# A graph kernel on one core: VectorE's sum of two edge types in three parts, and new places for the basis lots

## The chip, the cores and the metric

One Trainium2 chip, one NeuronCore. The time is device microseconds of one execution of the whole kernel, and the median of several executions is what versions are compared by.

## The reference

1536 nodes with 512 features, 26112 edges (`src`, `dst`, a type of 0 or 1, a weight), and four graph layers one after another, each followed by a residual and a layer norm:

```
layer 0: attention over image features, segment_sum of x[src] by dst, two products with W, relu
layer 1: two gated relational steps. For each type r: w[r] = sum over 30 bases of att[r, b] * basis[b],
         out = segment_sum(where(type == 0, gate0 * (x[src] @ w[0]), gate1 * (x[src] @ w[1])), dst) + x @ root + bias
layer 2: five GIN steps, relu((1 + e) * (h @ W) + A @ (h @ W) + b), then log_softmax
layer 3: support = x @ W, out = segment_sum(support[src] * weight, dst) + bias
```

The kernel turns each segment sum into a product with a dense 1536 x 1536 matrix: one of edge counts for each type, their sum for layers 0 and 2, and one of weights for layer 3.

## The kernel before, in words

The change lies in the first stage, which runs from about 20 us to about 320 us. It does two jobs side by side.

**Counting edges.** The 1536 destinations are cut into 96 windows of 16 (`W`), eight windows to a block of 128 (`PER`), twelve blocks (`BLOCKS`). The edges are sorted by destination, so a window needs a few tiles of 128 edges: two in static slots and one or two more in a loop with a count read from the data. For each tile VectorE writes one-hot matrices (`sources` L713, `source` L718, `keys` L722 and L723), and TensorE multiplies them (`counts`, L1483 and L1484) into one of three PSUM rings (`win`). Static slots are used by every second window, the looped slot `looped_slot(w)` too, so a window with a second looped tile needs its slot back from TensorE in the middle. ScalarE evicts a window's counts to `typed` (in the buffer `wb`, L1203) and its weights to `aw_stage` (L1205). When a block's eight windows are done, TensorE turns it in six lots ("turn" lots, L1460 and L1463), and ScalarE writes the turned tiles to `adj` and to `aw_dram`. Once a block VectorE adds both types of `typed` into `adj[:, 0]` (`sum_types`, L708); it does that in the window with index `RING` = 3 of the next block, behind that window's one-hots.

**Combining the bases.** Both relational steps need 2 x 512 x 512 weights from 30 bases. These stream in as 64 chunks of 960 KB (`load_chunk`, L382), and TensorE reduces each in a "basis" lot (L1451, eight matmuls); ScalarE copies every second result to `mixed`, SP writes it to DRAM. There are four chunk buffers (`basis_of`); two lie in rows of `adj` that the last blocks need, so from chunk 52 on only two are used. A chunk's buffer is loaded again by SP as soon as TensorE has read it (`follower`, `side_ps`). Chunks 53 to 63 wait for the chunk that is two before them, earlier ones for that four before.

**The order.** The lots of both kinds form one list `side`; `by_window[u]` says which lots TensorE and ScalarE do behind window u. Turn lots of block s stand in windows q = 1 to 6 of the next block. Basis lots stand in every window with `u % 3 != 2`, so at windows 0, 1, 3, 4, 6, 7 and so on. SP works through chunks in order. It also issues seven small loads (`small`: biases, `Wa`, `eps`), one with each of chunks 8 to 14. After all lots it loads `wf` into `wb`, behind waits for all lots and for all sums. ScalarE waits for the sum of block s - 2 before it overwrites that half of `typed` (`typed_summed`).

Behind the stage come the turned x, the attention, and then the products of the four layers, on TensorE almost without a gap.

Of the kernel before, what the change touches and what calls it, by code (L numbers as in the profile page):

```python
# [6 lines left out]
ALU, ACT, AX = mybir.AluOpType, mybir.ActivationFunctionType, mybir.AxisListType  # L7

P = 128
# [14 lines left out]
RING = 3  # L24
# [8 lines left out]
N_SMALL = 7  # L33
# [10 lines left out]
def program(nc, ins, out):  # L44
    with ExitStack() as ctx:
        def sb(name, shape, dt):
            return ctx.enter_context(nc.sbuf_tensor(name, shape, dt))

        def sem(name):
            return ctx.enter_context(nc.semaphore(name))  # L50


        adj = sb("adj", [P, 3, NT, N], F16)
# [109 lines left out]
        def lay(n, dt, shape_str=None, **kw):  # L163
            nonlocal at
            size = n * (2 if dt in (F16, BF16) else 4) // 2
            v = flat[:, at:at + size]
            at += size
            if dt != F16:
                v = v.bitcast(dt)
            return v.rearrange(shape_str, **kw) if shape_str else v  # L170
# [10 lines left out]
        basis = [flat[:, 0:4 * D * 2].bitcast(F32), lay(4 * D, F32)]  # L181
# [12 lines left out]
        def follower(n):  # L194

            return min([m for m in range(n + 1, 64) if basis_of(m) == basis_of(n)], default=None)
# [20 lines left out]
        def looped_slot(w):  # L217

            return 4 + w % 2

        def static_slots(w):

            return 2 * (w % 2), 2 * (w % 2) + 1
# [3 lines left out]
        typed = wb[:, :, :, :].rearrange("p a b n -> p (a b n)").bitcast(F16)[:, 0:2 * 2 * NT * P].rearrange("p (k m j d) -> p k m j d", k=2, m=2, j=NT)  # L227
        assert 2 * at <= H1 + 7 * 2048

        c_ready = sem("c_ready")  # L230
# [14 lines left out]
        typed_summed = sem("typed_summed")  # L245
# [3 lines left out]
        weights = {k: sem("in_" + k) for k in ("wf", "wi", "img", "wim", "small", "wn", "wt", "wbm", "bap", "ts_a", "ts_b", "ts_in", "root", "l1a", "l1b", "aw", "att", "as_out", "as_in")}  # L249
# [62 lines left out]
        BLOCKS = N // P  # L312
        PER = P // W
        CH = 2 * 32

        side, by_window = [], {u: [] for u in range(NW)}
        for u in range(NW):
            here = []
            s, q = u // PER - 1, u % PER
            if s >= 0 and 1 <= q <= 6:  # L320
                here += [("turn", s, q - 1)]
            if u == NW - 1:
                here += [("turn", BLOCKS - 1, n) for n in range(6)]
            if u % 3 != 2:
                n = 2 * (u // 3) + u % 3
                here.append(("basis", n // (CH // 2), n % (CH // 2)))
            for what in here:
                by_window[u].append((len(side),) + what)
                side.append(what)
        lot_of = {what: n for n, what in enumerate(side)}  # L330

        def evicted(w):

            return win_free[w % RING], w // RING + 2
# [17 lines left out]
        def side_copied(n):  # L352

            return len([m for m in range(n + 1) if leaves(m)])
# [20 lines left out]
        def _(sp):  # L375
# [3 lines left out]
            def load_chunk(n):  # L379
                l, c = n // (CH // 2), n % (CH // 2)  # L380
                c = c // 2 + 16 * (c % 2)
                sp.dma_start(basis[basis_of(n)][0:120, :], bases[l][:, c * (4 * D):(c + 1) * (4 * D)]).then_inc(basis_in[basis_of(n)], 16)  # L382

            sp.wait_ge(edges_in, 64)
            for n in range(3):
# [4 lines left out]
            small = [  # L390
                (bcol[:, 0:2], ins["L0_gnn_bf"].rearrange("(k p) -> p k", p=P)),
                (bcol[:, 2:4], ins["L0_gnn_bi"].rearrange("(k p) -> p k", p=P)),
                (bcol[:, 4:5], ins["L0_gnn_ba"].unsqueeze(0).broadcast_to([P, 1])),
                (wa[:, :], ins["L0_gnn_Wa"].rearrange("(k p) o -> p (k o)", p=P)),
                (epsc[:, 0:5], ins["L2_gnn_eps"].unsqueeze(0).broadcast_to([P, 5])),
                (bcols[:, 0, :], ins["L0_gnn_bn"].rearrange("(k p) -> p k", p=P)),
                (bcols[:, 1, :], ins["L0_gnn_bim"].rearrange("(k p) -> p k", p=P)),
            ]
            assert len(small) == N_SMALL
            FIRST_SMALL = 8  # L400

            def x_load(g):
                a, b = X_GROUPS[g]
                sp.dma_start(x_first[:, a:b, :], ins["x"][P * a:P * b, :].rearrange("(k p) d -> p k d", p=P)).then_inc(x_in[g], 16)

            for n in range(CH):
                l, c = n // (CH // 2), n % (CH // 2)
                lot = lot_of[("basis", l, c)]
                if n == FIRST_SMALL:
                    sp.wait_ge(c_ready, 8)  # L410
                if FIRST_SMALL <= n < FIRST_SMALL + N_SMALL:
                    to, of = small[n - FIRST_SMALL]
                    sp.dma_start(to, of, allow_slow_non_contiguous=True).then_inc(weights["small"], 16)
                if follower(n):
                    sp.wait_ge(side_ps, lot + 1)
                    load_chunk(follower(n))
                    if follower(n) == CH - 1:
                        x_load(2)
                if c % 2 == 0:
                    continue  # L420
                sp.wait_ge(side_out, side_copied(lot))
                m = n // 2
                for q in range(4):

                    sp.dma_start(combs[l][q, c // 2, :, :], mixed[m % 4][32 * q:32 * q + 16, :]).then_inc(comb_out[m % 4], 16)
# [6 lines left out]
            x_load(0)  # L432
            x_load(1)
            sp.wait_ge(side_ps, len(side))
            sp.wait_ge(typed_summed, BLOCKS)
            sp.dma_start(wf, ins["L0_gnn_Wf"].rearrange("(k p) n -> p k n", p=P)).then_inc(weights["wf"], 16)
            for k in range(4):
                sp.wait_ge(comb_out[k], 64 * 9)
# [181 lines left out]
        def _(dve):  # L620
# [30 lines left out]
            for f in range(2):  # L651
                for h in range(2):
                    k = 2 * (1 - f) + h
# [47 lines left out]
            def window(w):  # L701
                return dve.value_load(wrow_i[0:1, 0, w:w + 1], min_val=0, max_val=PACKED)  # L702

            def sum_types(s):

                for k in range(RING):
                    dve.wait_ge(*evicted(PER * s + PER - 1 - k))
                dve.tensor_tensor(adj[:, 0, :, P * s:P * s + P], typed[:, s % 2, 0, :, :], typed[:, s % 2, 1, :, :], ALU.add).then_inc(typed_summed, 1)  # L708

            dve.wait_ge(c_ready, 7)  # L710
            def sources(w, t):
# [16 lines left out]
            for w in range(NW):  # L728
                n, u = w // REL, w % REL
                if u == 0:  # L730
                    dve.wait_ge(krel_ready, n + 1)
                one, two = static_slots(w)
                dve.wait_ge(onehot_free[one], w // 2 + 1)
                dve.wait_ge(onehot_free[two], w // 2 + 1)
                sources(w, first)
                keys(one, first, n, u)
                if w + 1 < NW:
                    following = window(w + 1)
                keys(two, nc.s_assert_within(first + 1, 0, EC - 1, skip_runtime_bounds_check_because=why), n, u)
                with dve.Fori(0, steps) as q:  # L740
                    dve.wait_ge(onehot_free[looped_slot(w)], before + q + 1)
                    last = nc.s_assert_within(first + q + 2, 0, EC - 1, skip_runtime_bounds_check_because=why)
                    source(looped_slot(w), last)
                    keys(looped_slot(w), last, n, u)
                if w + 1 < NW:
                    first, steps, before = unpack(following)
                if w >= PER and w % PER == RING:
                    sum_types(w // PER - 1)
            sum_types(BLOCKS - 1)

            for n, i in enumerate(X_ORDER):
                if i == 6:
# [400 lines left out]
        def _(act):  # L1153
# [40 lines left out]
            for w in range(NW):  # L1194
                s, u, b = w // PER, w % PER, w % RING
                through = following
                if w + 1 < NW:
                    following = act.value_load(wrow_i[0:1, 2, w + 1:w + 2], min_val=1, max_val=NW * MOST)
                if u == 0 and s >= 2:
                    act.wait_ge(side_ps, staged_again(s))  # L1200
                    act.wait_ge(typed_summed, s - 1)
                act.wait_ge(onehot_free[looped_slot(w)], through + 1)
                act.activation(typed[:, s % 2, :, :, W * u:W * u + W],  # L1203
                               win[b][:, 0, 0:TW].rearrange("p (d m j) -> p m j d", d=W, m=2), ACT.Copy)
                act.activation(aw_stage[:, s % 2, :, W * u:W * u + W],  # L1205
                               win[b][:, 1, 0:AWW].rearrange("p (d j) -> p j d", d=W), ACT.Copy).then_inc(win_free[b], 1)
                if w % REL == REL - 1 and w // REL + 2 < NW // REL:
                    move_keys(w // REL + 2)
                for lot in by_window[w]:
                    side_lot(*lot)  # L1210
# [606 lines left out]
```

## Time and profile before

| what | value |
|---|---|
| median of 3 runs | 1824.29 us (1818.31 to 1826.46) |
| the profiled execution | 1819.87 us |
| its span | 1818.0 us |
| TensorE busy | 1755.0 us (97%) |
| VectorE busy | 874.1 us (48%) |
| ScalarE busy | 594.6 us (33%) |
| TensorE's granted clock, mean | 0.998 |

The span reaches from the first to the last instruction. The shares of busy time are averages over stages with different limits. The stage in question is the first sixth of the span, where the DMA engines move some 250 GB/s and VectorE is nearly as busy as TensorE.

### The profile page before, as it was taken

How to read it: one execution, taken by the hardware profiler on the slowest of the kernel's cores; microseconds unless marked ns; L12 is line 12 of the kernel's file. 1: busy time of each engine (PE TensorE's matmuls, PEld its weight loads, DVE VectorE, ACT ScalarE, POOL GpSimd, SP SyncE). 2: the span in 40 equal slices, each digit the busy share in tenths (PEclk: the TensorE clock that was granted, in tenths of full speed). 3: DMA queues.
4: the chain of work that ended last, by engine and by line, in shares of the span. 5: the costliest groups of instructions: out<-in, count | busy, mean ns of one | idle time of the engine just before them, and what ended most of it. 6: DMA issues, size and time to landing. Idle time of an engine off the chain costs nothing.

```text
span 1818.0 us, 22292 instructions
## 1 busy us (share of the span) xinstructions
PE 1755.0 (97%) x7318; PEld 849.4 (47%) x7318; DVE 874.1 (48%) x1890; ACT 594.6 (33%) x1232; POOL 10.8 (1%) x36
## 2 busy tenths in 40 slices
PE   5989888999999999999999999999999999999998
PEld 3556555533334444444444444444544444444444
DVE  7888787489885312112222224334253443594123
ACT  2555444566876311222110001232323323232000
POOL 1000000000000000000000000000000000000000
PEclk9999999999999999999999999999999999999999
DMA  7999979810302401000011116300000010021111
GB/s 182 273 254 263 267 230 237 327 36 1 145 24 81 168 2 46 0 1 23 0 47 35 35 35 241 147 0 30 1 0 30 1 41 1 1 84 56 35 47 47
DMA packets 45781, 157.80 MB, mean 87 GB/s; under 512 B 7686, under 2 KB 9630, under 8 KB 37094
## 3 DMA queue, kind: packets, MB, share of 16 engines
q1 hardware_dynamic: 43792, 146.95, 26.6%
q10 hardware_dynamic: 1878, 9.44, 1.4%
q8 instruction: 62, 1.02, 0.2%
q14 instruction: 49, 0.40, 0.1%
HBM read 120.71 MB, written 35.65 MB: 86 GB/s over the span
## 4 chain that ended last, share of the span: by engine, by line
PE 82%; DVE 7%; issue 3%; DMA 3%; DVEq 3%; ACT 1%; POOL 0%; POOLq 0%
PE psum L1556 31%; PE psum L1570 31%; PE psum L1797 7%; DMA hs<-in_L_gnn_basis 3%; PE psum L1747 2%; PE psum L1484 2%; PE psum L1451 2%; PE psum L1644 2%; PE psum L1631 1%; PE psum L1483 1%; PE psum L1522 1%; DVEq L702 1%; DVE hs L723 1%; DVE xt L723 1%; DVEq L723 1%
## 5 line engine op out<-in xcount | busy, mean ns | idle before, releaser
L1570 PE MATMUL psum<-hs,adj 128*128 128x512 f16 x2880 | 636.2, 379 | 0.0
L1556 PE MATMUL psum<-wb,xt 128*128 128x512 f32 x1056 | 457.7, 593 | 0.0
L1570 PEld LDWEIGHTS psum<-hs,adj 128*128 128x128 f16 x2880 | 281.2, 98 | 330.7 <-issue 11.0
L1556 PEld LDWEIGHTS psum<-wb,xt 128*128 128x128 f32 x1056 | 198.7, 190 | 245.3 <-issue 243.6
L1335 ACT ACTIVATE ua<-ua 128x512 f32<-128x512 f32 x60 | 37.9, 631 | 314.7 <-DVE ua L1113 181.0
L1109 DVE SCALAR_TENSOR_TENSOR vt<-psum,scl,xt 128x512 f32<-128x512 f32 x60 | 44.8, 746 | 192.7 <-PE psum L1570 192.7
L1044 DVE TENSOR_TENSOR vt<-psum,adj 128x512 f32<-128x512 f32 x24 | 16.6, 692 | 249.3 <-PE psum L1556 249.3
L1556 PE MATMUL psum<-adj,xt 128*128 128x512 f32 x288 | 130.1, 594 | 0.0
L1797 PE MATMUL psum<-hs,adj 128*128 128x512 f32 (+1 forms) x312 | 123.8, 559 | 0.0
L1323 ACT ACTIVATE lnst<-lnst,bcol 128x1 f32<-128x1 f32 x24 | 7.1, 295 | 280.1 <-DVE lnst L1022 270.5
L1036 DVE SCALAR_TENSOR_TENSOR hs<-psum,gates,hs 128x512 f16<-128x512 f32 x48 | 33.8, 747 | 120.9 <-ACT hs L1358 120.9
L1203 ACT ACTIVATE wb<-psum 128x384 f16<-128x384 f32 x96 | 47.2, 491 | 136.5 <-PE psum L1484 136.5
L1797 PEld LDWEIGHTS psum<-hs,adj 128*128 128x128 f32 x312 | 59.3, 190 | 64.8 <-issue 63.6
L1346 ACT ACTIVATE hs<-psum,scl 128x512 f16<-128x512 f32 x60 | 41.2, 687 | 136.5 <-PE psum L1556 127.0
L1102 DVE SCALAR_TENSOR_TENSOR xt<-psum,scl,hs 128x512 f32<-128x512 f32 x60 | 45.1, 751 | 82.5 <-ACT hs L1346 81.9
L1265 ACT ACTIVATE adj<-hs,pbias 128x512 f32<-128x512 f32 x108 | 69.2, 712 | 45.7 <-DVE adj L890 45.7
L1556 PEld LDWEIGHTS psum<-adj,xt 128*128 128x128 f32 x288 | 53.8, 190 | 60.2 <-issue 56.7
L1484 PE MATMUL psum<-hs 128*128 128x192 f32 x296 | 73.3, 330 | 0.0
L1358 ACT ACTIVATE hs<-psum,gates 128x512 f16<-128x512 f32 x48 | 30.4, 684 | 119.6 <-PE psum L1556 119.6
L1483 PE MATMUL psum<-hs 128*128 128x384 f16 x148 | 49.4, 334 | 18.0 <-DVE hs L723 17.8
L1138 DVE TENSOR_TENSOR vt<-psum,hs 128x512 f32<-128x512 f32 x11 | 7.6, 692 | 106.6 <-PE psum L1797 106.6
L1318 ACT ACTIVATE xt<-psum 128x512 f32<-128x512 f32 x84 | 48.7, 580 | 22.1 <-PE psum L1747 22.1
(256 smaller groups left out, 1880.7 us busy)
## 6 DMA issues: line engine op xcount, KB each, us to landing
hs<-in_L_gnn_basis SPq DMA_DIRECT2D x38, 960.0 KB, 10.3
adj<-in_L_gnn_basis SPq DMA_DIRECT2D x26, 960.0 KB, 11.8
aw_scratch<-xt ACTq DMA_DIRECT2D x12, 768.0 KB, 10.1
adj<-aw_scratch SPq DMA_DIRECT2D x1, 9216.0 KB, 37.1
x_scratch<-adj SPq DMA_DIRECT2D x24, 256.0 KB, 2.3
hs<-x_scratch SPq DMA_DIRECT2D x24, 256.0 KB, 2.6
ts_scratch<-adj SPq DMA_DIRECT2D x2, 2304.0 KB, 19.5
as_scratch<-adj SPq DMA_DIRECT2D x1, 4608.0 KB, 16.8
```

Of the source, the lines that this page charges most:

```text
L723: dve.tensor_scalar(onehot_w[k], iota_s[:, AWW * u:AWW * u + AWW], krel[:, n % 2, 1, bass.ds(t, 1)], ecol[:, 3, bass.ds(t, 1)], ALU.is_equ ...
L1102: dve.scalar_tensor_tensor(own(i), psum[:, U_BANK[i % 3], :], scl[:, 2:3], kit["bb"][:, r % 2, :], ALU.mult, ALU.add)
L1109: step(dve.scalar_tensor_tensor(vt[:, :], psum[:, i % 2, :], scl[:, 1:2], own(i), ALU.mult, ALU.add))
L1203: act.activation(typed[:, s % 2, :, :, W * u:W * u + W], win[b][:, 0, 0:TW].rearrange("p (d m j) -> p m j d", d=W, m=2), ACT.Copy)
L1265: x = act.activation(second[:, g, :], proj[:, 1, 512 * c:512 * c + 512], ACT.Tanh, bias=pbias[:, 1, 9 * g + a:9 * g + a + 1])
L1318: act.activation(xt[:, i, :, :].rearrange("p k n -> p (k n)"), psum[:, 7, :], ACT.Copy).then_inc(t_cp, 1)
L1346: act.activation(hs[:, 0, 0, i, :], psum[:, U_BANK[i % 3], :], ACT.Copy, scale=scl[:, 0:1]).then_inc(u_hi, 1)
L1483: pe.matmul(win[b][:, 0, 0:TW], onehot_s16[k], onehot_t[k], start=first, stop=True, skip_group_check=True)
L1484: pe.matmul(win[b][:, 1, 0:AWW], onehot_s[k], onehot_w[k], start=first, stop=True, skip_group_check=True).then_inc(onehot_free[k], 1)
L1556: x = pe.matmul(psum[:, bank, :], xt[:, i, k, :], w[:, k, :], start=first and k == 0, stop=last and k == 3)
L1570: x = pe.matmul(psum[:, i % 2 + (4 * half if own else 0), :], adj[:, m, j, P * i:P * i + P], hs[:, t, half, j, :], start=n == 1 or (own an ...
L1797: x = pe.matmul(psum[:, bank, part_of], aw[:, j, P * i:P * i + P], sup[:, j, part_of], start=j == 0, stop=j == NT - 1)
```

## The change

The sum of a block becomes three instructions over four of the twelve rows `j` each, behind the one-hots of windows 3, 4 and 5 of the next block; the counts that others wait for are three times as high. The seven small loads are issued right behind chunk 3, before the loop over chunks, and the wait for `c_ready` in front of them goes. The places of the basis lots are fixed by block: in the block of windows in which block s is turned, q = 0, 2, 4, 5, 6, 7 where s is a multiple of three (s = -1 stands for the first eight windows, in which nothing is turned), else q = 0, 2, 4, 6, 7, and q = 0, 2, 4, 5, 6 in the last. That gives 64 lots as before.

```diff
--- before.py
+++ after.py
@@ -321,8 +321,9 @@
                 here += [("turn", s, q - 1)]
             if u == NW - 1:
                 here += [("turn", BLOCKS - 1, n) for n in range(6)]
-            if u % 3 != 2:
-                n = 2 * (u // 3) + u % 3
+            at_q = (0, 2, 4, 5, 6) if s == BLOCKS - 2 else (0, 2, 4, 6, 7) if s % 3 else (0, 2, 4, 5, 6, 7)
+            if q in at_q:
+                n = len([what for what in side if what[0] == "basis"])
                 here.append(("basis", n // (CH // 2), n % (CH // 2)))
             for what in here:
                 by_window[u].append((len(side),) + what)
@@ -397,7 +398,8 @@
                 (bcols[:, 1, :], ins["L0_gnn_bim"].rearrange("(k p) -> p k", p=P)),
             ]
             assert len(small) == N_SMALL
-            FIRST_SMALL = 8
+            for to, of in small:
+                sp.dma_start(to, of, allow_slow_non_contiguous=True).then_inc(weights["small"], 16)
 
             def x_load(g):
                 a, b = X_GROUPS[g]
@@ -406,11 +408,6 @@
             for n in range(CH):
                 l, c = n // (CH // 2), n % (CH // 2)
                 lot = lot_of[("basis", l, c)]
-                if n == FIRST_SMALL:
-                    sp.wait_ge(c_ready, 8)
-                if FIRST_SMALL <= n < FIRST_SMALL + N_SMALL:
-                    to, of = small[n - FIRST_SMALL]
-                    sp.dma_start(to, of, allow_slow_non_contiguous=True).then_inc(weights["small"], 16)
                 if follower(n):
                     sp.wait_ge(side_ps, lot + 1)
                     load_chunk(follower(n))
@@ -432,7 +429,7 @@
             x_load(0)
             x_load(1)
             sp.wait_ge(side_ps, len(side))
-            sp.wait_ge(typed_summed, BLOCKS)
+            sp.wait_ge(typed_summed, 3 * BLOCKS)
             sp.dma_start(wf, ins["L0_gnn_Wf"].rearrange("(k p) n -> p k n", p=P)).then_inc(weights["wf"], 16)
             for k in range(4):
                 sp.wait_ge(comb_out[k], 64 * 9)
@@ -701,11 +698,13 @@
             def window(w):
                 return dve.value_load(wrow_i[0:1, 0, w:w + 1], min_val=0, max_val=PACKED)
 
-            def sum_types(s):
-
-                for k in range(RING):
-                    dve.wait_ge(*evicted(PER * s + PER - 1 - k))
-                dve.tensor_tensor(adj[:, 0, :, P * s:P * s + P], typed[:, s % 2, 0, :, :], typed[:, s % 2, 1, :, :], ALU.add).then_inc(typed_summed, 1)
+            def sum_types(s, third):
+
+                if third == 0:
+                    for k in range(RING):
+                        dve.wait_ge(*evicted(PER * s + PER - 1 - k))
+                js = slice(4 * third, 4 * third + 4)
+                dve.tensor_tensor(adj[:, 0, js, P * s:P * s + P], typed[:, s % 2, 0, js, :], typed[:, s % 2, 1, js, :], ALU.add).then_inc(typed_summed, 1)
 
             dve.wait_ge(c_ready, 7)
             def sources(w, t):
@@ -744,9 +743,10 @@
                     keys(looped_slot(w), last, n, u)
                 if w + 1 < NW:
                     first, steps, before = unpack(following)
-                if w >= PER and w % PER == RING:
-                    sum_types(w // PER - 1)
-            sum_types(BLOCKS - 1)
+                if w >= PER and RING <= w % PER < RING + 3:
+                    sum_types(w // PER - 1, w % PER - RING)
+            for third in range(3):
+                sum_types(BLOCKS - 1, third)
 
             for n, i in enumerate(X_ORDER):
                 if i == 6:
@@ -1198,7 +1198,7 @@
                     following = act.value_load(wrow_i[0:1, 2, w + 1:w + 2], min_val=1, max_val=NW * MOST)
                 if u == 0 and s >= 2:
                     act.wait_ge(side_ps, staged_again(s))
-                    act.wait_ge(typed_summed, s - 1)
+                    act.wait_ge(typed_summed, 3 * (s - 1))
                 act.wait_ge(onehot_free[looped_slot(w)], through + 1)
                 act.activation(typed[:, s % 2, :, :, W * u:W * u + W],
                                win[b][:, 0, 0:TW].rearrange("p (d m j) -> p m j d", d=W, m=2), ACT.Copy)
```

## Rows read from the trace of the kernel before

**Rows 1.** Engines by stretch: busy us (instructions), PEclk, DMA share, GB/s.
```profile
20.00:50.00 30.00, 25.17 (x144) 13.87 (x145) 24.68 (x84) 10.54 (x27) 0.00 (x0) 1.00 0.86 208
50.00:180.00 130.00, 120.26 (x855) 74.74 (x853) 111.60 (x373) 70.09 (x165) 0.00 (x0) 1.00 0.96 264
180.00:205.00 25.00, 18.55 (x135) 12.36 (x133) 17.58 (x60) 11.33 (x27) 0.00 (x0) 1.00 0.96 264
...
262.00:318.00 56.00, 46.42 (x313) 28.80 (x313) 41.03 (x139) 25.62 (x60) 0.00 (x0) 0.97 0.92 240
```

**Rows 2.** Groups of DVE instructions by form, 14 to 320 us.
```profile
L722 DVE TENSOR_SCALAR hs<-hs 128x384 f16<-128x384 f16 x148 | 46.8, 316 | 8.4 <-issue 4.5
...
L708 DVE TENSOR_TENSOR adj<-wb 128x1536 f16<-128x1536 f16 x12 | 11.4, 953 | 4.2 <-ACT xt L1205 3.9 <-issue 0.2
```

**Rows 3.** DVE in order of time, 222 to 230.5 us: start, us, line.
```profile
222.17 0.43 DVE L713 TENSOR_TENSOR xt<-hs 128x256 f32<-128x256 f16 x1
...
224.32 0.37 DVE L723 TENSOR_SCALAR looped<-hs 128x192 f32<-128x192 f16 x1
224.60 0.95 DVE L708 TENSOR_TENSOR adj<-wb 128x1536 f16<-128x1536 f16 x1
225.47 0.42 DVE L713 TENSOR_TENSOR hs<-hs 128x256 f32<-128x256 f16 x1
...
227.57 0.43 DVE L713 TENSOR_TENSOR xt<-hs 128x256 f32<-128x256 f16 x1
...
230.18 0.42 DVE L713 TENSOR_TENSOR hs<-hs 128x256 f32<-128x256 f16 x1
```

**Rows 4.** Who waited for whom, 14 to 320 us: us in total, times, longest.
```profile
DVE looped L718 <- PE psum L1484: 15.4, 6, 5.2
...
PE psum L1451 <- DMA hs<-in_L_gnn_basis: 7.2, 7, 2.4
...
DVE hs L718 <- PE psum L1484: 5.0, 4, 1.4
...
PE psum L1451 <- DMA adj<-in_L_gnn_basis: 2.1, 2, 1.3
```

**Rows 5.** DVE in order of time, 296 to 298 us, idle before in brackets.
```profile
297.34 0.29 DVE L718 TENSOR_SCALAR looped<-hs 128x128 f32<-128x128 f16 x1 [5.04 <-PE psum L1484]
```

**Rows 6.** Line L382, the basis loads, 128 to 200 us.
```profile
  PE psum L1451: 4.5, 4
...
DMA to landing us min/median/max: 10.8/16.3/18.4
```

**Rows 7.** Line L382, 262 to 320 us.
```profile
DMA to landing us min/median/max: 6.6/8.5/10.2
```

**Rows 8.** Chain of waits, 240 to 320 us: start, us, what.
```profile
250.90 0.99 PE psum L1451 x8
...
253.96 1.00 PE psum L1451 x8
...
264.22 8.79 DMA hs<-in_L_gnn_basis
...
283.07 1.10 PE psum L1451 x8
...
292.90 1.76 PE psum L1451 x8
...
305.06 1.04 PE psum L1451 x8
306.12 8.32 DMA hs<-in_L_gnn_basis
...
314.58 1.06 PE psum L1451 x8
```

**Rows 9.** Line L413, the small loads.
```profile
DMA to landing us min/median/max: 8.1/8.8/10.7
```

**Rows 10.** PE in order of time, at 279.7 us.
```profile
279.74 1.06 PE L1451 MATMUL psum<-hs,attw 120*32 120x512 f32 x8
```

## The prediction

> **What bounds the kernel now.** I first read the page: PE is busy 97% of the span, but nearly all of that lies behind the first stage, which the change does not touch. So the first stage (from 20 us to the last turned tile near 320 us) is read by itself, in stretches [rows 1]. No engine is full there: between 50 and 180 us PE is busy 120.3 of 130 us, DVE 111.6, the DMA engines 96%. Who sets the pace is seen in DVE's order of time [rows 2, 3]. A window with three tiles and no sum takes DVE 2.61 us from one L713 to the next (227.57 to 230.18), and the starts follow one another without any wait for another engine. What DVE waits for [rows 4] confirms it: ten waits for PE in 300 us, 20.4 us together. There are ten windows with a second looped tile, whose slot has to come back from PE, and each waits about 1.0 to 1.5 us. Two of them waited 5 us (one is in [rows 5], the other is the longest of [rows 4]); about 3.8 us of each is more than their like. Behind these two stands a basis chunk that had not landed: PE waited for L1451's data 7 times on buffers in hs and twice in adj [rows 4]. So the stage has two limits close together: DVE's pace, and the time in which a freed basis buffer is full again.
>
> That second time has two regimes. With four buffers a load takes 16.3 us in the median between 128 and 200 us [rows 6], while the DMA engines are 96% busy, and four buffers are used once in six windows (15.7 us at 2.61, some 17.5 with the two-step windows). With two buffers (chunks 53 to 63) it takes 6.6 to 10.2 us, median 8.5 [rows 7], and a buffer is used again after three windows. There the chain itself runs over loads: 264.22 to 294.66 is load, chunk, load, chunk, load, chunk, and again 306.12 to 314.58 [rows 8].
>
> **The change, part by part.**
>
> *The sum in three parts.* Twelve TENSOR_TENSORs of 128x1536 f16 at 0.95 us [rows 2] become 36 of 128x512. The trace has no such form. From below stands the 128x384 f16 L722 with 0.32 us, from above L713, 0.42 us in [rows 3]; I take 0.40. An instruction overlaps the next by about 0.08 (the sum takes 0.95, its successor starts after 0.87), so a third holds DVE for 0.32 and three for 0.96. What counts is the pace. The window with the sum is 3.30 us (222.17 to 225.47), but the one behind it only 2.10 [rows 3]: while the long instruction runs, the queue prepares addresses and loads values ahead, and 0.51 us of gaps vanish from the next window. One sum thus costs 3.30 + 2.10 - 2 x 2.61 = 0.18 us. A third of 0.32 can hide 0.32 of such gaps in each of three windows, so three cost 0 to 0.1. For the eleven sums within the loop this is 11 x 0.18 = 2.0 us less at best; I take -1.7. If a third hid nothing, it would be 3 x 0.32 - 0.18 = +0.78 a block, +8.6 in all: the upper bound. The last block's three stand behind the loop; wf waits for them, but also for PE's last turned tile, which comes some 3 us later, so 0.1 us there is covered (0.1 if the cover were gone). ScalarE's wait for the sums is met two windows later than before, still three windows before it is needed: nothing.
>
> The Trainium skill ("VectorE: DVE Perf Modes", the section on the TRN2 errata) speaks against this part: each SBUF instruction pays a fixed cost of about 150 cycles, and many small tiles pay it each time. By it 24 more instructions would be an estimated 24 x 0.156 = 3.7 us more instead of 1.7 less. The two rows of [rows 3] show that busy time is not what a sum costs here.
>
> *Small loads sooner.* Seven issues leave SP's loop over chunks 8 to 14 and stand behind chunk 3. SP has no wait to miss there: after chunk 3 it waits for PE's first basis lot anyway, and the DMA engines are 86% busy in 20 to 50 us against 96% later [rows 1]. Each landed in 8.1 to 10.7 us [rows 9], and nobody waits for them before 320 us. The bytes are few, the elements small. Taking them out of a stretch in which PE never waited for a chunk is worth 0 to 1 us; I take -0.3. Were they to delay chunks 2 or 3 by their whole 10.7 us, those would land near their use; hence above 0 I keep 1 us.
>
> *Lots in fixed stretches.* The number of lots is the same (64 in 96 windows), so the work of PE, ScalarE and DMA is. What moves is their distance. Before, chunks stood at windows 0, 1, 3, 4, 6, 7, ...: four buffers always came round in six windows, two in three. Now blocks have five or six chunks; q=4, 5, 6, 7 and the next block's q=0 follow at once. Three effects.
>
> (a) PE. A window with a turn and a basis lot takes PE 3.06 us (250.90 to 253.96 in [rows 8]), 0.45 over DVE's 2.61. Three in a row instead of two put it 1.3 us back instead of 0.9. DVE has slots for two windows, and with 0.9 it never waited outside two-step windows (the ten waits of [rows 4]). I take 0; the upper bound is 4 such blocks x 0.4 = 1.6. Two-step windows gain or lose a lot just before them about equally often (windows 46 and 23 gain, 16 and 63 lose): 0.
>
> (b) Four buffers. Most chunks are used one window later than before (0 to 2 windows, and 0 for the last chunk of a six-block and those just behind it). Where the DMA engines are the limit (chunks 28 to 43), landings stay and uses move back 2.6 us, so PE's four waits there, 4.5 us [rows 6], shrink; but chunk 43 stays at window 64, and what was not lost before it has to be waited for there. I take -1 us (0 to -3.8, the whole surplus of the 5.2 us wait). Against this, chunks 11, 27 and 43 have only four windows from buffer to buffer instead of six. 4 x 2.9 - 1.1 is 10.5 us; loads there can be a little faster, as fewer are in flight. +0.3 for chunk 27; if it took the 16.3 of [rows 6], +5.8.
>
> (c) Two buffers. Here it costs. New places of chunks 53 to 63: windows 80, 82, 84, 85, 86, 87, 88, 90, 92, 93, 94 (before 79, 81, 82, 84, 85, 87, 88, 90, 91, 93, 94). From window 84 five chunks follow in five windows, on two buffers, two windows (5.2 us) apart. Step by step with 8.5 us for a load and 1.06 for the lot: chunk 55 takes the place of 56 in window 84, 279.7 to 280.8 [rows 10]; 56 that of 57, 283.1 to 284.1 [rows 8]. 57 could start at 286.1, but lands at 280.8 + 8.5 = 289.3, ends 290.4. 58 lands 292.6, ends 293.7. 59 lands 290.4 + 8.5 = 298.9, ends 300.0. Before, the same chunk in the same window ended at 294.66 [rows 8]: +5.3 us. Then 61, now in window 92: w91's lot stood at 305.06, so about 308.0 + 5.3 = 313.3, less about 1 since fewer lots run at the lower clock (0.97 in 262 to 318 [rows 1]; the lot at 292.90 took 1.76 instead of 1.06 behind a wait), ends 313.4; chunk 63 takes the same buffer and lands at 313.4 + 8.5 = 321.9, against 314.4 now [rows 8]. PE is ready for it before (313.2 + 5.3 = 318.5 at the latest). That is +7.5 us at the end of the stage, by which everything behind is moved. With the fastest load (6.6) the same steps give 63 at 317.3, +2.7; with the slowest (10.2) 328.1, +13.5.
>
> Nothing behind the stage changes; its parts start when turned tiles and loads are there.
>
> **The sum.** -1.7 (thirds) -0.3 (small) -0.7 (four buffers, net) +7.5 (two buffers) = +4.8 us. The profiled execution took 1819.87 us (span 1818.0 and 1.9 around it); so it would take 1825. It stands 4.4 us below the median of the runs, 1824.29; carried to that, 1829.
>
> **Rivals.**
>
> *Slow loads.* With two buffers each load takes about 10.2 us as chunk 60's did, and chain (c) gives +13.5 and in sum +10.8: 1835. For it: 59, 61 and 63 share the engines with comb writes and x. Against it: median 8.5. It decides from about 9.7 us a load. Chance 0.15, with the case that chunk 27 waits its 5.8 us (1834).
>
> *Thirds pay in full.* The hidden gaps are gone: +8.6 in place of -1.7, 1838. For it: a third of 0.32 is shorter than the 0.51 of gaps. Against it: the gaps are short pieces, 0.1 to 0.3 each, and any cover hides them. Chance 0.06. The Trainium skill's fixed cost would end between, at about 1834 by the estimate above.
>
> *Faster.* The waits for chunks go altogether: both long DVE waits lose their surplus (3.8 + 3.7) and the last PE wait of 1.4, with the thirds' 1.7 that is -10.6: 1814. It needs chunks two windows apart to be in time, that is loads of 4.2 us or less with two in flight; the shortest row is 6.6. Or, short of that, that PE and DVE catch up later what chain (c) loses; they can by 1.6 us a light window only where no load is awaited. Chance 0.08.
>
> *Nothing.* The burst in windows 84 to 88 is covered by the slack before and behind it, and the rest cancels: 1824. Against it: the chain already runs over loads here. Chance 0.09.
>
> *My forecast* has 0.62, its own range is 1822 to 1834.
>
> **Numbers.** 1829 us. A change within 0.5% (9.1 us) can't be told from none here: the three runs already spread over 8 us. Faster by more (under 1815.2): 0.08. Slower by more (over 1833.4): the two slow rivals, 0.21. Between: 0.71. The range takes in half of the faster rival's distance and the slow rivals up to 1838: 1817 to 1838.
>
> **What would show it.** Thirds: window lengths on DVE of 2.6 to 2.7 us at q=3, 4, 5 instead of 3.30 and 2.10. Buffers: PE's waits for L1451's data (7.2 and 2.1 us now [rows 4]) fall around 180 to 200 us and rise in windows 86 to 88 and at the last chunk, with the chain over loads from about 280 us. The last basis lot near 322 instead of 314.6, against which thirds and four buffers set 2 to 3 us. The prediction is wrong if loads in the burst land in less than 6.6 us, or if DVE's windows no longer sit at 2.61.

## The result, and the profile after

The changed kernel takes 1832.32 us in the median of 5 runs (1829.35 to 1832.94), the kernel before 1821.89 us in 5 runs (1818.31 to 1826.46). The ratio is 1.0045, with a 95% interval of 1.0025 to 1.0065: some 8 us slower (4.6 to 11.8), where +4.8 was forecast. The two medians alone lie 10.4 us apart. Its profiled execution took 1829.35 us, span 1827.5.

The stretches of the stage after, in the columns of [rows 1]:

```profile
20.00:50.00 30.00, 25.63 (x143) 14.12 (x144) 24.63 (x84) 10.61 (x27) 0.00 (x0) 1.00 0.86 191
50.00:180.00 130.00, 116.36 (x825) 72.41 (x822) 108.75 (x372) 68.47 (x161) 0.00 (x0) 1.00 0.96 261
180.00:205.00 25.00, 22.10 (x153) 13.43 (x152) 20.39 (x70) 12.22 (x29) 0.00 (x0) 1.00 0.96 263
262.00:318.00 56.00, 43.02 (x271) 26.54 (x269) 35.84 (x123) 21.10 (x49) 0.00 (x0) 0.88 0.85 212
```

Until 262 us there is little to see; between 180 and 205 us PE and DVE are even busier than before, since the long wait of the old trace fell into it. The last stretch differs: DVE 35.8 us busy instead of 41.0, PE 43.0 instead of 46.4, DMA 85% instead of 92%, and the granted clock 0.88 instead of 0.97. Fewer things run at the same time.

The chain of waits of the changed kernel, 240 to 332 us (start, us, what), against [rows 8]:

```profile
261.81 8.35 DMA hs<-in_L_gnn_basis
...
270.29 1.60 PE psum L1451 x8
...
284.58 6.99 DMA hs<-in_L_gnn_basis
...
291.71 1.10 PE psum L1451 x8
292.83 10.05 DMA hs<-in_L_gnn_basis
...
303.02 1.93 PE psum L1451 x8
...
319.27 7.01 DMA hs<-in_L_gnn_basis
...
326.41 1.07 PE psum L1451 x8
```

Four times in these rows a basis load stands in it, with a lot right behind. The chain before had four as well [rows 8], so it is not their number that differs but when the lots behind them start. The lot of chunk 63 starts at 326.41 instead of 314.58, 11.8 us later. In front of it stands what the closer places did (PE in order of time, idle before in brackets, and DVE's wait in window 89, which was 5.04 us in [rows 5]):

```profile
270.29 1.60 PE L1451 MATMUL psum<-hs,attw 120*32 120x512 f32 x8 [1.90 <-DMA hs<-in_L_gnn_basis]
...
291.71 1.07 PE L1451 MATMUL psum<-hs,attw 120*32 120x512 f32 x8 [2.18 <-DMA hs<-in_L_gnn_basis]
...
296.75 1.07 PE L1451 MATMUL psum<-hs,attw 120*32 120x512 f32 x8 [2.40 <-DMA hs<-in_L_gnn_basis]
...
303.02 1.93 PE L1451 MATMUL psum<-hs,attw 120*32 120x512 f32 x8 [2.42 <-DMA hs<-in_L_gnn_basis]
...
326.41 1.07 PE L1451 MATMUL psum<-hs,attw 120*32 120x512 f32 x8 [2.15 <-DMA hs<-in_L_gnn_basis]
```

```profile
308.11 0.29 DVE L717 TENSOR_SCALAR looped<-hs 128x128 f32<-128x128 f16 x1 [11.37 <-PE psum L1484]
```

PE waits for chunks 57, 58, 59 one after another, and again for 63. The first of these rows comes before the burst: chunk 53 stands in window 80 now, and chunk 51, whose buffer it takes, moved from window 76 to 78, so these two are only two windows apart as well. PE waited 1.90 us for it, where the kernel before did not wait for chunk 53 at all. In window 89 VectorE stands still for 11.37 us, because its looped slot comes back only when PE is through with all of that. Who waited for whom, 14 to 332 us, against [rows 4]:

```profile
DVE looped L717 <- PE psum L1484: 17.5, 6, 11.4
PE psum L1451 <- DMA hs<-in_L_gnn_basis: 14.2, 7, 2.4
...
DVE hs L717 <- PE psum L1484: 7.0, 4, 2.5
...
PE psum L1451 <- DMA adj<-in_L_gnn_basis: 0.3, 1, 0.3
```

The ten waits of DVE on slots sum to 24.5 instead of 20.4 us, PE's waits for chunks to 14.5 instead of 9.3. Most of the latter come late (line L383, the basis loads, that was L382: first 128 to 200 us, then 262 to 330 us; against [rows 6, 7]):

```profile
  PE psum L1451: 3.2, 2
...
DMA to landing us min/median/max: 11.8/15.4/18.2
...
  PE psum L1451: 11.0, 5
...
DMA to landing us min/median/max: 7.0/7.8/10.1
```

11.0 of the 14.5 us lie behind 262 us. What became of the sum (DVE in order of time; L707 is the third, L712 a window's first instruction, against [rows 3]):

```profile
223.87 0.42 DVE L712 TENSOR_TENSOR xt<-hs 128x256 f32<-128x256 f16 x1
...
226.31 0.42 DVE L707 TENSOR_TENSOR adj<-wb 128x512 f16<-128x512 f16 x1
226.66 0.43 DVE L712 TENSOR_TENSOR hs<-hs 128x256 f32<-128x256 f16 x1
...
227.23 0.37 DVE L722 TENSOR_SCALAR hs<-hs 128x192 f32<-128x192 f16 x1
227.75 0.32 DVE L721 TENSOR_SCALAR hs<-hs 128x384 f16<-128x384 f16 x1
...
229.44 0.42 DVE L712 TENSOR_TENSOR xt<-hs 128x256 f32<-128x256 f16 x1
...
230.41 0.32 DVE L721 TENSOR_SCALAR xt<-hs 128x384 f16<-128x384 f16 x1
...
232.35 0.42 DVE L712 TENSOR_TENSOR hs<-hs 128x256 f32<-128x256 f16 x1 [0.17 <-issue]
```

And behind the stage (the chain again, 326 to 358 us, then line L433, the load of Wf, that was L436):

```profile
330.98 7.29 DMA hs<-in_x
...
338.31 2.40 PE psum L1475 x20
340.71 3.70 PE psum L1522 x8
```

```profile
DMA to landing us min/median/max: 6.0/6.0/6.0
```

The last lot is 11.8 us late, but the first product L1522 starts at 340.71 instead of 331.17, only 9.5 late. In both traces it starts as soon as Wf has landed: issued at 322.85 and landed at 331.13 before, issued at 334.69 and landed at 340.66 now. The issue stands 8.3 us behind the start of the last lot in both; what differs is that Wf took 5.97 instead of 8.28 us, and that is the whole 2.3 us. The span grew by 9.5 us.

### The profile page after: what moved, and what is told of

It reads as the page before. It is cut to its first block, busy times and chain, and to the rows that moved or that the text cites. A ratio compares the mean times of both kernels' runs of the same rounds, so it can differ in the third digit from the quotient of the medians.

```text
span 1827.5 us, 22316 instructions
## 1 busy us (share of the span) xinstructions
PE 1761.2 (96%) x7318; PEld 851.1 (47%) x7318; DVE 876.1 (48%) x1914; ACT 594.4 (33%) x1232; POOL 10.8 (1%) x36
## 4 chain that ended last, share of the span: by engine, by line
PE 81%; DVE 8%; issue 4%; DVEq 3%; DMA 3%; ACT 1%; POOL 0%; SPq 0%; POOLq 0%; ACTq 0%
PE psum L1556 31%; PE psum L1570 31%; PE psum L1797 7%; DMA hs<-in_L_gnn_basis 3%; PE psum L1747 2%; PE psum L1644 2%; PE psum L1631 1%; PE psum L1484 1%; PE psum L1451 1%; DVEq L699 1%; PE psum L1522 1%; DVE hs L722 1%; PE psum L1483 1%; DVEq L722 1%; DVE xt L722 1%
## 5 line engine op out<-in xcount | busy, mean ns | idle before, releaser
L1451 PE MATMUL psum<-hs,attw 120*32 120x512 f32 x304 | 42.8, 635 | 14.2 <-DMA hs<-in_L_gnn_basis 14.2
```

The costliest lines, as they stand in the source:

```text
L1451: x = pe.matmul(bank[32 * v:32 * v + 32, :], attw[0:120, a, 1 - h:33 - h], basis[basis_of(c)][0:120, D * v:D * v + D], start=h == 0, stop= ...
```

## The experiments

Each was timed in five rounds against the kernel before on the same chip (e1 to e4 on one chip, e5 to e8 and e9 to e11 on two others). "Ratio" is that to the kernel before.

| run | edit | median us | ratio (95%) |
|---|---|---|---|
| e1 | thirds alone | 1822.29 | 1.0006 (0.9990 to 1.0022) |
| e2 | small loads alone | 1818.71 | 0.9985 (0.9973 to 0.9997) |
| e3 | new lot places alone | 1831.20 | 1.0052 (1.0037 to 1.0067) |
| e4 | changed kernel, old places from window 72 | 1823.24 | 1.0002 (0.9990 to 1.0015) |
| e5 | before, new places up to window 71 | 1821.42 | 0.9990 (0.9975 to 1.0005) |
| e6 | changed kernel, third late buffer | 1822.68 | 0.9996 (0.9983 to 1.0010) |
| e7 | before, third late buffer | 1823.23 | 1.0004 (0.9988 to 1.0021) |
| e8 | before, 5 and 3 buffers, first chunks and small loads sooner | 1815.82 | 0.9967 (0.9948 to 0.9985) |
| e9 | before, small loads twice | 1826.02 | 1.0025 (1.0012 to 1.0039) |
| e10 | e7, extra load later | 1818.23 | 0.9973 (0.9957 to 0.9988) |
| e11 | e8 with new places up to window 71 | 1814.84 | 0.9953 (0.9937 to 0.9969) |

Theory 1: the chunks' reload chain on two buffers, which the burst in windows 84 to 88 makes too short, costs nearly all. Theory 2: the thirds cost it. Theory 3: the bursts on four buffers cost it.

**One part at a time.** e1 takes the `sum_types` lines of the diff alone, e2 the lines on `small`, e3 those on `at_q`.

> The kernel before with the sum in three parts alone. The changed kernel's own windows q=3 to 6 add to 0.15 us more per block than before's. Theory 1 (the reload chain on two buffers costs nearly all): +1 to +3 us against before. Theory 2 (each third pays in full): +8 us. The prediction's own step said -1.7.

> The kernel before with the small loads right behind chunk 3 alone. Theory 1: 0 to -0.5 us, within the noise. Rival: if the small elements delayed the first chunks or the instruction fetch, +1 us or more.

> The kernel before with the new places of the basis lots alone. Theory 1: +7 to +9 us, PE's wait for a chunk in windows 86 to 88 and VectorE's wait of about 11 us in window 89 as in the changed kernel. Theory 2: 0 to +2. Theory 3 (the bursts on four buffers cost as much): +7 to +9 too, but VectorE is already 3 us or more late at window 80.

With 1822 us as base the three ratios are +1.1, -2.7 and +9.5 us, sum +7.9; the change as a whole was +8.2. So they add up as well as intervals of 2 to 4 us to either side can show it, and the places of the lots are the loss. Theory 2 falls with e1: +8 us is outside its interval, which ends at +4.0. e2's -2.7 is more than either reading had said. e3 shows the same picture as the changed kernel, with 8.7 us instead of 11 for VectorE's wait in window 89. PE in order of time and who waited for whom, in e3:

```profile
297.90 1.93 PE L1452 MATMUL psum<-hs,attw 120*32 120x512 f32 x8 [3.08 <-DMA hs<-in_L_gnn_basis]
```

```profile
DVE looped L719 <- PE psum L1485: 15.9, 6, 8.7
PE psum L1452 <- DMA hs<-in_L_gnn_basis: 13.4, 10, 3.1
```

The sign named for theory 3 is in this trace too: VectorE begins window 80 at 3.8 us later than in the trace before. But it is 2.6 us late there in e1's trace and 5.1 in e2's, which have the old places, so this sign separates nothing; e4 and e5 have to.

**Which lots.** e4 is the changed kernel with

```diff
-            if q in at_q:
+            if (q in at_q if u < 72 else u % 3 != 2):
```

and e5 the kernel before with the new places under the same condition. In both layouts 48 chunks stand before window 72, so the two halves fit together.

> The changed kernel with the basis lots of the last three blocks of windows (from window 72, chunk 48) at their old places. Theory 1: only 0 to +2.5 us over before, so 6 to 8 us of the loss gone. Theory 2 or 3: still +6 to +8 us over before.

> The kernel before with the new lot places up to window 71 alone, the last three blocks as before. If the parts add up (lots 9.5, old tail 8): +1 to +2.5 us over before. If the bursts on four buffers cost nothing: 0.

e4 is at 1.0002: with the old tail the loss is gone, so 1.0045 - 1.0002, some 8 us, sits in the last three blocks. e5 is at 0.9990: 72 windows of new places cost nothing that can be seen, their interval ends at +0.9 us, below the +1 to +2.5 of the first reading. Theory 3 falls. The last three blocks hold the burst and chunk 53 alike, and no run tells the two apart.

**Is it the buffers?** The places are what e4 changed; a third buffer leaves them alone. e6 and e7 use a piece of `hs` that is free until x is loaded:

```diff
+        basis.append(part(hflat, H1 + 14336, [4 * D]))
...
-            return (n + 1) % 4 if n < FAR_CHUNKS else (n + 1) % 2
+            return (n + 1) % 4 if n < FAR_CHUNKS else (0, 4, 1)[n % 3]
...
+                if n == EXTRA_SOON:
+                    load_chunk(FAR_CHUNKS)
```

with `EXTRA_SOON` = 44, and `x_load(2)` behind chunk 61.

> The changed kernel, its lot places untouched, with a third chunk buffer for chunks 52 to 63 (in a part of hs that is free until x is loaded). Theory 1 (a buffer has two windows to be full again): the burst is served, -7 to -10 us against the changed kernel, so 1822 to 1825, VectorE's wait in window 89 back to 1 to 2 us. Rival (the DMA engines' rate is what the burst lacks, or the half clock of PE): under 3 us gained, PE still waits over 2 us for chunks 57 to 59.

> The kernel before with the same third buffer. Theory 1: the waits for chunks 55 to 63 go, and VectorE's 5.0 us in window 89 falls to about 1.3: -4 to -6 us. Rival (DMA rate): 0 to -2.

e6 makes good 1.0045 - 0.9996 = 0.0049, 9 us, with the burst still there: theory 1 stands, in its wider form that a buffer has two windows to be full again. Its rival said under 3. But its second sign missed: DVE's wait in window 89 did not fall to 1 to 2 us (DVE and PE in e6, in order of time):

```profile
296.51 1.34 PE L1455 MATMUL psum<-hs,attw 120*32 120x512 f32 x8 [2.37 <-DMA hs<-in_L_gnn_basis]
```

```profile
300.95 0.28 DVE L721 TENSOR_SCALAR looped<-hs 128x128 f32<-128x128 f16 x1 [5.53 <-PE psum L1488]
```

Chunk 59 was still late, by 2.37 us, and before it chunk 48, by 2.80 at 241.8 us, behind the extra load. For chunks 53, 57, 58 and 63 PE no longer waited. e7 missed altogether: no gain. PE in e7, in order of time:

```profile
250.77 1.94 PE L1455 MATMUL psum<-adj,attw 120*32 120x512 f32 x8 [3.85 <-DMA adj<-in_L_gnn_basis]
```

The extra load of 960 KB, issued at 227.8 us into full DMA engines, made chunk 49 late, and PE waited 3.85 us. Against the trace before, VectorE lost 4.8 us between windows 72 and 80 and gained 4.1 between windows 89 and 90: the wait was moved forward, not removed. e10 issues it with chunk 48's reload instead:

```diff
-        EXTRA_SOON = 44
+        EXTRA_SOON = 48
```

> e7 with the extra chunk's first load issued with chunk 48's reload instead of four chunks sooner. If e7 gained nothing because that load of 960 KB delayed chunk 49 (PE waited 3.85 us for it): no wait for chunk 49, -3 to -5 us against before. Rival (three buffers bring nothing on before's places): 0.

0.9973, 4.9 us less than before, and PE waits for no chunk in adj (where chunk 49 lay) behind 182 us. Who waited for whom in e10, 14 to 332 us:

```profile
DVE looped L722 <- PE psum L1488: 10.6, 6, 3.4
...
PE psum L1455 <- DMA hs<-in_L_gnn_basis: 5.2, 5, 2.3
...
PE psum L1455 <- DMA adj<-in_L_gnn_basis: 2.7, 3, 1.3
```

So the kernel before also lost by its two buffers, though less than the changed one. That the later issue is what freed this gain rests on the trace above all: the intervals of e7 and e10 meet at 0.9988.

**The small loads.** e2's gain was nine times my term. Instead of moving them, e9 issues them twice, the second time with chunks 15 to 21 into spare room:

```diff
...
+                if FIRST_SMALL + N_SMALL <= n < FIRST_SMALL + 2 * N_SMALL:
+                    to, of = twice[n - FIRST_SMALL - N_SMALL]
+                    sp.dma_start(to, of, allow_slow_non_contiguous=True).then_inc(weights["again"], 16)
```

> The kernel before, with the seven small loads issued a second time with chunks 15 to 21, into spare room. If the small loads cost 2.7 us where they stand (what e2 seemed to show by moving them): +2 to +3 us. If e2's gain was a matter of when the chunks happen to land: 0 to +1.

+4.6 us (1.0025), more than either reading. A second set costs (2.2 to 7.1 us by its interval), the first set's move saves (0.5 to 4.9): seven loads of 10 KB in all weigh some microseconds where chunks stream. Who waited for whom in e9:

```profile
PE psum L1458 <- DMA hs<-in_L_gnn_basis: 10.7, 12, 2.3
...
PE psum L1458 <- DMA adj<-in_L_gnn_basis: 5.0, 6, 1.8
```

In this trace PE waited 18 times for a chunk instead of 9, first at 80 us, where the kernel before had no such wait until 183. But that can't be put down to the second set: e1's trace, with the small loads where they were, has 16 such waits, the first at 90 us, and e2's, with the small loads gone from there, has 13. Why so few bytes weigh so much isn't settled. It is not the time in which SP issues them (some 0.4 us each): from chunk 12 to chunk 29 each reload is issued 0.06 us behind the lot that it waits for, in the traces of before, e2 and e9 alike, but for one in e9 at 1.16 us. The DMA engines are 96 to 98% busy in 60 to 130 us in each version. e9's stream moves 254 GB/s there against 270 before, but in e2 it is 259, and a single trace can't tell the part of the small loads from what differs between executions anyway.

**A version that beats both.** e8 has five buffers up to chunk 51 (`(n + 1) % 5`), three behind, the whole sum and the small loads sooner, and issues chunk 3 ahead of two waits and chunk 4 in its old place; e11 has the new places up to window 71 as well.

> The kernel before with small loads sooner, five buffers up to chunk 51 and three behind. If the waits around 200 us come from too few buffers: the 5.2 us wait goes as well, 1811 to 1814. If they come from the DMA rate (16 us landings at 96% busy): only e7's gain and the 2.7 us of the small loads, 1814 to 1817.

> e8 with the new lot places up to window 71. If they are worth nothing by themselves with buffers enough: as e8, 1816 (0.997 of before). If the second of e5's readings (0.999) is real: 1 to 2 us less than e8.

0.9967 and 0.9953, 6.0 and 8.6 us under the kernel before; against each other they can't be told apart. e8's median, 1815.82, lies in the range of its second reading (1814 to 1817) and not of the first. Who waited for whom in e8, in the fastest of its executions (1810.36):

```profile
DVE looped L717 <- PE psum L1483: 7.8, 6, 1.8
...
DVE hs L717 <- PE psum L1483: 4.4, 4, 1.4
...
PE psum L1450 <- DMA hs<-in_L_gnn_basis: 0.7, 1, 0.7
```

The ten waits of DVE are down to 12.2 us, little over 1 us each: what a second looped tile costs by itself. PE waited once for a chunk, 0.7 us. So with five buffers the waits around 200 us can be absent. That they are absent as a rule is not shown: e11's trace, with as many buffers, has waits of 2.34 and 0.81 us for chunks 26 and 27 at 142 to 147 us, and e10's and e2's gains (4.9 and 2.7 us) together already exceed the 6.0 of e8. What the fifth buffer is worth before chunk 52 stays open.

## Why the prediction came out as it did

The direction, the place and the mechanism of the loss were right, and the range held the time. Whether the change is over 0.5% can't be said: the ratio's interval is 1.0025 to 1.0065. That the sum came within 3.4 us of the ratio's 8.2 is in part luck: the thirds missed by +2.8 and the small loads by -2.4, and these two cancel. Two sums of the text were off as well. Thirds in full are +8.6 in place of -1.7, so +15.1 in all and 1839, not 1838. And the bounds of the two-buffer term (+2.7, +13.5) leave out the 1 us for the clock that its middle takes off; with it they are +1.6 and +12.4.

**Thirds (forecast -1.7, measured +1.1, interval -1.8 to +4.0).** By time alone the forecast isn't refuted; the window lengths refute it. The step that failed is that a third hides as much of the gaps as it lasts. The windows are 2.79 us (223.87 to 226.66), 2.78 and 2.91 (with an irregular gap of 0.24 us), not 2.6 to 2.7. A third lasts 0.42 and not 0.40, and holds DVE for 0.35 (226.31 to 226.66) and not 0.32. Behind the first third the gap of 0.19 in front of the next window is gone (without a sum that window starts 0.47 behind the last instruction, 229.71 to 230.18 in the trace before, where 0.28 would do), but the later gaps of that window are at full size (226.66 to 227.75 is 1.09, as in a window without a sum in front). Behind the second, 0.12 more is gone (229.44 to 230.41 is 0.97). Three times 0.35 less 0.19 and twice 0.31 gives an estimate of 0.24 a block, against 0.18 for the whole sum. Where nothing waits, the four windows from q=3 on take some 0.08 us more (from window 19 to window 23: 10.78 in e1, 10.70 in e2), so 0.9 us over eleven blocks and not 1.7 less. The rival "thirds pay in full" (+8.6) gave too much. So did, as a cost of the path, the Trainium skill's fixed cost per instruction ("VectorE: DVE Perf Modes", TRN2 errata), whose estimate of +3.7 is above the 0.9 of the windows, though within the interval of the time. The third's own duration agrees with that page: by its figures, a fixed 0.156 us and 256 cycles at 0.96 GHz, an estimate is 0.42 us. I took the gaps for one reservoir; they are several small ones, and a third reached one or two of them.

**Small loads (forecast -0.3, measured -2.7, interval -4.9 to -0.5).** The failing step is that a delay was priced at next to nothing because it falls "in a stretch in which PE never waited for a chunk". That was so in one trace; e1's trace, with the same places of lots and small loads, has such waits soon behind it, from 90 us on. In the trace before, chunk 22 landed 9.0 us ahead of its use at 123.2 us and chunk 35 only 0.3 us ahead at 177.4, so a delay near 80 us could have been paid near 190. That this is how the small loads cost is not shown: in e2's trace, from which they are gone, chunk 18 already lands 0.1 us ahead of its use. That trace is of one of e2's slowest executions (1822.71), so it can't show the gain. What the loads do to the stream stays open.

**Lots, PE and four buffers (forecast -0.7, measured with e5 -1.8, interval -4.6 to +0.9).** Nothing here contradicts the forecast, and its parts can't be told apart. In the changed kernel's trace PE waited 1.54 and 1.62 us for chunks 27 and 28, where I had put 0.3, and the long wait near 200 us was gone.

**Lots, two buffers (forecast +7.5, measured some 8, by trace 10.3).** At window 80 DVE was 1.5 us later than before, at chunk 63 PE was 11.8 later, so the tail lost 10.3 us. The largest part that the sum leaves out is chunk 53. My steps began with window 84 on time, at 279.7; its lot started at 283.46, 3.7 us late, 2.2 of them since window 80. I had not seen that chunk 53, in window 80, comes only two windows behind chunk 51, and PE waited 1.90 us for it (1.39 in e3's trace, and in none of the traces with that chunk at window 79). From there to window 88 the steps held better: +5.3 forecast, 6.6 more in the trace. A load took 8.5 us in the sum; the load of chunk 59 took 10.05, within the bound I had for it. And I took 1 us off for the clock, while it went the other way. In the changed kernel's trace, by stretch:

```profile
262.00:298.00 36.00, 27.04 (x181) 16.43 (x180) 26.63 (x91) 14.66 (x35) 0.00 (x0) 0.95 0.89 229
298.00:306.00 8.00, 5.58 (x21) 2.94 (x20) 0.00 (x0) 1.31 (x3) 0.00 (x0) 0.50 0.93 219
```

From 298 to 306 us, behind two waits of over 2 us, the granted clock was at its lower level (1.2 GHz), and chunk 59's lot took 1.93 instead of 1.06. The kernel before had a shorter such stretch, 0.68 from 294 to 298 us, and the same lot took 1.76 in it, so this lot by itself adds little. The waits in the burst came out near the steps in sum, not one by one: by my steps 3.2, 0.7, 3.6 and 3.4 us for chunks 57, 58, 59 and 63, in the trace 2.2, 2.4, 2.4 and 2.2. What I had not counted is the wait for chunk 53, and that PE runs slowly for longer.

**What stands behind the stage.** "By which everything behind is moved" was right as far as the change goes. The trace gave 2.3 us back there, but only because its load of Wf took 5.97 us instead of 8.28. That differs from execution to execution: it took 5.64 us in e1's trace and 9.67 in e6's, and in every one of these traces the first product L1522 starts within 0.2 us of Wf's landing. So these 2.3 us are no term of the change. The tail's 10.3 us by trace and its 8 by time agree within the intervals of the changed kernel and e4, which leave some 4 us to either side.

## What to carry to other kernels

Where work with buffers is laid out by hand, write down for each buffer the distance from one use to the next, in time, beside the load's duration with its neighbours in flight. The number per block may be the same and the time still lost, if the shortest distance shrinks under the load. Look for every pair of uses at the short distance, not for the visible burst alone: here the first pair, chunks 51 and 53, stood ahead of it. A prefetch put into full DMA engines can move a wait instead of taking it away (e7, e10).

## What the runs showed that I had not expected

Seven small loads of 10 KB in all cost some 3 to 5 us among streaming chunks and nothing that can be seen right behind the start (e2, e9). There, behind the first four chunks, they took even longer to land in the changed kernel, 11.8 us in the median instead of 8.8 [rows 9]:

```profile
DMA to landing us min/median/max: 7.5/11.8/12.6
```

Executions of nearly the same program differ by several microseconds in the middle of the stage: e7 and e10 have the same instructions up to chunk 44, and DVE reaches window 40 at 142.33 us in one and at 138.28 in the other. Where a chunk is late is not a property of the kernel alone, so single traces were read here for how, and the times of many executions for how much.

The granted clock fell to its lower level behind two waits of 2.18 and 2.40 us on PE, in a stretch in which PE was otherwise three quarters busy (0.50 from 298 to 306 us, named above). In e7 it was at 0.50 from 250 to 254 us, behind the wait of 3.85 us, and the lot took 1.94 us.
